# A cross-attention and FP4 feed-forward layer on one core: the down projection in three f32r products, and the low part of x subtracted by GpSimd

## What is computed

```python
def fp4_quant_dequant(x):             # blocks of 16 along the last dim
    scale = max(abs(block)) / 6.0 ; xn = block / scale
    return _GRID[searchsorted(_MID, abs(xn))] * sign(xn) * scale
def fp4_linear(x, w):
    return einsum('bsk,nk->bsn', fp4_quant_dequant(x), fp4_quant_dequant(w))

x = x + attention(layernorm(x), ctx, ctx, bias, mask, in_proj, out_proj)
x = x + fp4_linear(silu(fp4_linear(ln, w_gate)) * fp4_linear(ln, w_up), w_down)   # ln = layernorm(x)
```

## Time and profile before

| | |
|---|---|
| median of 3 runs | 930.79 us |
| the profiled execution | 930.9 us, span 928.9 us |
| PE busy | 883.6 us, 95% |
| DVE busy | 710.6 us, 76% |
| ACT busy | 617.8 us, 67% |
| POOL busy | 534.8 us, 58% |
| granted TensorE clock | 0.993 on average |

### The profile page before, as it was taken

The page is one execution under the profiler, slowest core; times in us unless marked ns, Lnnn a source line. Parts: engine busy times, 40 slices in busy tenths (PEclk is TensorE's granted clock), DMA queues, the critical chain, the costliest instruction groups (busy, mean ns, idle before and its releaser), DMA issues.

```text
span 928.9 us, 20211 instructions
## 1 busy us (share of the span) xinstructions
PE 883.6 (95%) x6772; PEld 706.7 (76%) x6772; DVE 710.6 (76%) x1866; ACT 617.8 (67%) x1119; POOL 534.8 (58%) x501
## 2 busy tenths in 40 slices
PE   5699999999999999999999999999889999999997
PEld 5577777787777777777787777777568888888886
DVE  3868678677677776776776679899579999989984
ACT  2377677777677776777776777787755555555542
POOL 5677867776696687677678557875203222222222
PEclk9799999999999999999999999999999999999999
DMA  6577334442442534344243343610000000000000
GB/s 193 150 221 205 113 72 126 103 117 71 114 116 60 146 86 102 98 100 132 74 115 103 72 134 73 174 35 1 1 1 12 18 18 19 21 17 17 18 18 29
DMA packets 50796, 76.50 MB, mean 82 GB/s; under 512 B 5264, under 2 KB 22032, under 8 KB 50704
## 3 DMA queue, kind: packets, MB, share of 16 engines
q1 hardware_dynamic: 50448, 75.06, 29.9%
q10 hardware_dynamic: 256, 0.26, 0.1%
HBM read 45.16 MB, written 29.36 MB: 80 GB/s over the span
## 4 chain that ended last, share of the span: by engine, by line
PE 79%; ACT 6%; issue 6%; DVE 4%; POOL 2%; DMA 2%; SPq 1%; ACTq 0%; DVEq 0%
PE psum L1233 26%; PE psum L1377 11%; PE psum L1331 11%; PE psum L1584 9%; PE psum L1569 4%; PE psum L1568 4%; PE psum L1567 4%; PE psum L1295 3%; PE psum L1255 2%; ACT att L776 2%; DVE att L1089 2%; PE psum L1261 2%; ACT att L783 1%; PE psum L1272 1%; ACT att L727 1%
## 5 line engine op out<-in xcount | busy, mean ns | idle before, releaser
L1089 DVE CUSTOM_DVE_ANT_0 att<-psum,att 128x512 f32<-128x512 f32 x512 | 341.7, 686 | 143.3 <-PE psum L1331 141.4
L618 POOL TENSOR_TENSOR att<-att,neg_max 128x512 f32<-128x512 f32 x308 | 322.4, 1057 | 172.8 <-DVE neg_max L1089 170.4
L1233 PE MATMUL psum<-ident,att 128*128 128x128 f32 x2576 | 380.8, 276 | 25.2 <-ACT att L776 8.2
L1233 PEld LDWEIGHTS psum<-ident,att 128*128 128x128 f32 x2576 | 311.6, 142 | 93.0 <-ACT att L776 30.2
L776 ACT ACTIVATE att<-psum 128x512 f32<-128x512 f32 x512 | 298.3, 599 | 117.7 <-PE psum L1233 113.4
L1331 PE MATMUL psum<-stack 128*128 128x512 f32 x512 | 251.2, 492 | 10.5 <-DMA stack<-q_hl 7.2
L783 ACT ACTIVATE att<-att,neg_max 128x512 f32<-128x512 f32 x204 | 147.2, 722 | 13.4 <-DVE neg_max L1089 13.4
L701 POOL TENSOR_TENSOR att<-att 128x704 f32<-128x704 f32 x32 | 61.8, 1931 | 162.8 <-DVE att L1211 162.8
L1331 PEld LDWEIGHTS psum<-stack 128*128 128x128 f32 x512 | 97.8, 191 | 43.9 <-issue 32.3
L1377 PE MATMUL psum<-att 128*32 128x256 f32 x2048 | 123.8, 382 | 0.0
L1584 PE MATMUL psum<-att 128*128 128x256 f32 x384 | 91.7, 380 | 2.7 <-ACT att L903 2.7
(11 more groups left out here) (104 smaller groups left out, 1066.3 us busy)
## 6 DMA issues: line engine op xcount, KB each, us to landing
stack<-qk_planes SPq DMA_DIRECT2D x124, 192.0 KB, 3.9
qk_planes<-k_hl SPq DMA_DIRECT2D x48, 256.0 KB
qk_planes<-q_hl SPq DMA_DIRECT2D x48, 256.0 KB
att<-in_fside_1xSxS_dram SPq DMA_DIRECT2D x32, 256.0 KB, 2.8
att<-in_ctx_dram SPq DMA_DIRECT2D x8, 512.0 KB, 7.4
out_dram<-att SPq DMA_DIRECT2D x32, 128.0 KB, 1.7
x<-in_x_dram SPq DMA_DIRECT2D x1, 2560.0 KB, 13.5
x<-in_x_dram SPq DMA_DIRECT2D x3, 512.0 KB, 6.5
```

The costliest lines, as they stand in the source:

```text
L618: pool.tensor_tensor(prob[:, slot, :], prob[:, slot, :], neg_max[:, slot:slot + 1].to_broadcast([P, S]), ALU.subtract).then_inc(less_pool, 1)
L1089: dve.tensor_tensor_reduce(out=prob[:, slot, :], in0=ps_score[:, SCORE_BANK[2 * S_ + r], :], in1=bias_m[:, tt, :], scale=-1.0, scalar=BIG, ...
L1233: return pe.transpose(out_, in_, ident[:, :])
```

## The change

Down is now made in three f32r products like gate and up: 18 matmuls of 128x256 in place of six float32 chunks. For that, h gets a high and a low part: ACT copies PSUM twice, once rounded (into `hqT_hl`, in a slot of `stack` that attention has left), once in float32 (`f_hT`), and POOL subtracts. The down weights get a low part too, made by DVE (`weights_low`) from the three down pieces, in the place of `k_hl` and a longer `kv_hl`. The matmul with the negated identity is gone; instead ACT copies transposed x twice and POOL subtracts as well. PE transposes x of the next tile in the middle of gate and up, behind twelve of the 18 matmuls. The ring `prob` goes from 13 to 12 slots. Names of semaphores, buffer sizes and asserts are left out of the diff.

```diff
-    RING = 13
+    RING = 12
...
+        w_dn_high = kv_hl[:, AT_DN:AT_DN + IC * E].rearrange("p (c e) -> p c e", c=IC)
+        w_dn_low2 = kv_hl[:, AT_DN + IC * E:].rearrange("p (c e) -> p c e", c=2)
+        w_dn_low4 = k_hl.rearrange("p a s -> p (a s)").rearrange("p (c e) -> p c e", c=IC - 2)
+        def w_dn_low(c):
+            return w_dn_low4[:, c, :] if c < IC - 2 else w_dn_low2[:, c - IC + 2, :]
...
+        f_hT = cut(IC * P)
...
+        f_x32 = cut(E)
...
+        hqT_hl = stack[:, (2 * N_OCT - 1) % SLOTS, :, :, :].rearrange("p x k s -> p (x k s)").rearrange(
+            "p (i j n) -> p i j n", i=2, j=2)
...
-            pool.memset(w_dnT[:, IC - 1, :], 0.0).then_inc(vv_zero, 1)
+            pool.memset(kv_hl[:, 4 * EC * S:].bitcast(F32), 0.0).then_inc(vv_zero, 1)
...
             batches(pool, body)
+            def step(n, par):
+                m = n - 3
+                if live(m):
+                    pool.wait_ge(fhT_taken, m + 1)
+                    wait(pool, fdn_ready, m - 1)
+                    pool.tensor_tensor(hqT_hl[:, 1 - par, 1, :], f_hT, hqT_hl[:, 1 - par, 0, :].bitcast(F32),
+                                       ALU.subtract).then_inc(fhlow_ready, 1)
+                m = n - 2
+                if live(m):
+                    pool.wait_ge(fhd_ready, m + 1)
+                    if isinstance(m, int) and m == 0:
+                        pool.wait_ge(fgu_ready, 1)
+                        pool.memset(f_hq[:, :, I:IC * P], 0.0)
+                    wait(pool, fhT_ready, m - 1)
+                    pool.tensor_tensor(blocks(f_hq[:, par, 0:I]), blocks(f_hu), spread(f_s[:, 1 - par, 0:NHB], NHB),
+                                       ALU.mult).then_inc(fhq_ready, 1)
+                m = n + 1
+                if live(m):
+                    pool.wait_ge(fxT_taken, m + 1)
+                    pool.tensor_tensor(f_xqT_low[:, 1 - par, :, :].rearrange("p c t -> p (c t)"), f_x32,
+                                       f_xqT_high[:, 1 - par, :, :].rearrange("p c t -> p (c t)").bitcast(F32),
+                                       ALU.subtract).then_inc(fxlow_ready, 1)
+            ffn_head(step, -2, -1, 0)
             rstd2_of(B - 1)
-            def step(n, par):
-                m = n - 2
-                if not live(m):
-                    return
-                pool.wait_ge(fhd_ready, m + 1)
-                if isinstance(m, int) and m == 0:
-                    pool.wait_ge(fgu_ready, 1)
-                    pool.memset(f_hq[:, :, I:IC * P], 0.0)
-                wait(pool, fhT_ready, m - 1)
-                pool.tensor_tensor(blocks(f_hq[:, par, 0:I]), blocks(f_hu), spread(f_s[:, 1 - par, 0:NHB], NHB),
-                                   ALU.mult).then_inc(fhq_ready, 1)
-            ffn_loop(pool, step)
+            ffn_loop(pool, step, 1)
...
-                act.activation(f_xqT_high[:, par, :, :], ps_x[:, 0:E].rearrange("p (c t) -> p c t", c=EC),
-                               ACT.Copy).then_inc(fxT_taken, 1)
-            def x_low(m, par):
-                act.wait_ge(fxlow_made, m + 1)
-                act.activation(f_xqT_low[:, par, :, :], ps_x[:, 0:E].rearrange("p (c t) -> p c t", c=EC),
-                               ACT.Copy).then_inc(fxlow_ready, 1)
+                act.activation(f_xqT_high[:, par, :, :], ps_x[:, 0:E].rearrange("p (c t) -> p c t", c=EC), ACT.Copy)
+                wait(act, fxlow_ready, m)
+                act.activation(f_x32, ps_x[:, 0:E], ACT.Copy).then_inc(fxT_taken, 1)
...
-                    act.activation(f_hqT[:, 1 - par, :, :].rearrange("p c t -> p (c t)"), ps_h[:, 0:IC * P], ACT.Copy).then_inc(fhT_taken, 1)
+                    if isinstance(m, int) and m == 0:
+                        act.wait_ge(score_ready, TILES * N_OCT)
+                    act.activation(hqT_hl[:, 1 - par, 0, :], ps_h[:, 0:IC * P], ACT.Copy)
+                    wait(act, fhlow_ready, m)
+                    act.activation(f_hT, ps_h[:, 0:IC * P], ACT.Copy).then_inc(fhT_taken, 1)
...
+                if g == 2:
+                    src = bank.rearrange("p (c n) -> p c n", c=2)
+                    if m < IC - 2:
+                        dve.wait_ge(k_plane, 48 * N_OCT)
+                        dve.tensor_tensor(w_dn_low4[:, m:m + 2, :], src, w_dn_high[:, m:m + 2, :].bitcast(F32), ALU.subtract).then_inc(gw_low, 1)
+                    else:
+                        dve.tensor_tensor(w_dn_low2[:, 0, :], src[:, 0, :], w_dn_high[:, m, :].bitcast(F32), ALU.subtract)
+                        dve.tensor_tensor(w_dn_low2[0:ILAST, 1, :], src[0:ILAST, 1, :], w_dn_high[0:ILAST, m + 1, :].bitcast(F32),
+                                          ALU.subtract).then_inc(gw_low, 1)
+                    return
...
+            def x_transposes(m, par):
+                if not live(m):
+                    return
+                pe.wait_ge(fxq_ready, m + 1)
+                wait(pe, fxT_taken, m)
+                for c in range(EC):
+                    last = transposes(ps_x[:, c * P:(c + 1) * P], f_xq[:, 1 - par, c * P:(c + 1) * P])
+                last.then_inc(fxT_ready, 1)
             def ffn_step(n, par):
                 m = n - 3
                 if live(m):
@@ -1569,32 +1606,24 @@
                             last = pe.matmul(ps_gu[:, c0:c1], f_xqT_low[:, par, c, :], w_gu_high[:, c, c0:c1], start=False, stop=c == EC - 1)
                         if c0 < I <= c1:
                             last.then_inc(fgate_ready, 1)
+                            x_transposes(n + 1, par)
                     last.then_inc(fgu_ready, 1)
-                m = n + 1
-                if live(m):
-                    pe.wait_ge(fxq_ready, m + 1)
-                    wait(pe, fxlow_ready, m)
-                    for c in range(EC):
-                        last = pe.matmul(ps_x[:, c * P:(c + 1) * P], f_xq[:, 1 - par, c * P:(c + 1) * P], ident[:, :],
-                                         start=c == 0, stop=False, is_transpose=True, skip_group_check=True)
-                    last.then_inc(fxT_ready, 1)
-                def down(m, chunks):
-                    for c in chunks:
-                        last = pe.matmul(ps_y[:, 1 - par, :], f_hqT[:, 1 - par, c, :], w_dnT[:, c, :],
-                                         start=c == 0, stop=c == IC - 1)
-                    return last
+                elif live(n + 1):
+                    x_transposes(n + 1, par)
                 if live(n - 3):
                     pe.wait_ge(fhT_taken, n - 2)
                     wait(pe, fout_ready, n - 3)
-                    down(n - 3, range(0, IC // 2))
-                if live(m):
-                    pe.wait_ge(fxT_taken, m + 1)
-                    pe.matmul(ps_x[:, 0:E], neg_ident[:, :], f_xqT_high[:, 1 - par, :, :], start=False, stop=True,
-                              skip_group_check=True).then_inc(fxlow_made, 1)
-                if live(n - 3):
-                    down(n - 3, range(IC // 2, IC)).then_inc(fdn_ready, 1)
+                    for c in range(IC):
+                        high = hqT_hl[:, 1 - par, 0, c * P:(c + 1) * P]
+                        pe.matmul(ps_y[:, 1 - par, :], high, w_dn_high[:, c, :], start=c == 0, stop=False)
+                        pe.matmul(ps_y[:, 1 - par, :], high, w_dn_low(c), start=False, stop=False)
+                    pe.wait_ge(fhlow_ready, n - 2)
+                    for c in range(IC):
+                        last = pe.matmul(ps_y[:, 1 - par, :], hqT_hl[:, 1 - par, 1, c * P:(c + 1) * P], w_dn_high[:, c, :],
+                                         start=False, stop=c == IC - 1)
+                    last.then_inc(fdn_ready, 1)
```

More of the change, by code:

```diff
@@ L86, in xattn_ffn @@
         neg_half = sb("neg_half", [P, NT])
-        att = sb("att", [P, 28352])
+        att = sb("att", [P, 26816])
         used = [0]
@@ L121, in xattn_ffn @@
         oT = cut(EC, S)
-        at_w_dn = used[0]
-        w_dnT = cut(IC, E)
+        w_qT = cut(EC, E)
         w_outT = cut(EC, E)
@@ L126, in xattn_ffn @@
         bo_bc = cut(E)
-        w_qT = att[:, at_w_dn:at_w_dn + EC * E].rearrange("p (c e) -> p c e", c=EC)
         w_nat = probT.rearrange("p a b c d -> p (a b c d)")[:, 0:8 * E].rearrange("p (c e) -> p c e", c=8)
@@ L142, in xattn_ffn @@
         mean_var_b = sb("mean_var_b", [P, NT, 2])
-        neg_ident = sb("neg_ident", [P, P], F32R)
         var_eps2 = sb("var_eps2", [P, NT])
@@ L158, in xattn_ffn @@
         w_gu_high = stack[:, (2 * N_OCT - 3) % SLOTS, :, :, :].rearrange("p x k s -> p (x k s)")[:, 0:EC * GU].rearrange("p (c n) -> p c n", c=EC)
-        kv_hl = sb("kv_hl", [P, 4 * EC * S], F32R)
+        AT_DN = EC * GU
+        kv_hl = sb("kv_hl", [P, AT_DN + (IC + 2) * E], F32R)
         ctxT_high, ctxT_low, w_kv_high, w_kv_low = (
             kv_hl[:, i * EC * S:(i + 1) * EC * S].rearrange("p (c s) -> p c s", c=EC) for i in range(4))
-        assert 2 * E == S and EC * GU <= 4 * EC * S
+        assert 2 * E == S and 4 * EC * S <= AT_DN + (IC + 2) * E
```

(27 more changed lines are left out.)

2 lines of the change are left out of this document (removed).

## The result

The changed kernel takes 962.17 us (median of 4 runs, 961.45 to 962.32), the kernel before 930.84 us on the same chip (4 runs, 929.17 to 931.35). The ratio is 1.0338 [1.032, 1.0356]: 31 us slower. The forecast was 959.0 us, in a range of 938 to 972, with a chance of 0.88 for slower. The profiled execution took 962.24 us, its span 960.4 us.

What follows compares the result with a forecast made beforehand. The prediction took the chain through PE, ACT, POOL and DVE, 8.24 us a tile, as the bound. 930.9 us plus 23.2 for 28 tiles, 3.7, 1.9 and -1 gave 958.7, stated as 959, range 938 to 972.

Steps and rivals of the forecast that it cites:

- The mechanism: Feed-forward loop: POOL and DVE instructions with two SBUF operands hold each other, making the tile 8.24 us, 0.83 more.
- The chain, step by step: Feed-forward tile, from h's transposes over ACT's copies, POOL's subtraction, DVE and POOL's multiplication to the next transposes: 8.24 us.
- PE's sum: PE's own work in a feed-forward tile: 7.41 - 0.31 - 2.40 + 2.16 + 0.09 = 6.95 us.
- the split into 0.31 for L1594 and 2.40 for the float32 products: PE's down stretch: time freed by removing the negated-identity matmul (0.31 us) and the float32 down (2.40 us).
- the 0.09 us for a change of kind: PE, gate and up: transposes of x placed among the matmuls cost one more switch of kind, 0.09 us a tile.
- 28 x 0.83 = 23.2: Feed-forward loop: 28 tiles at the full pitch, each 0.83 us longer than before, add 23.2 us.
- The tail: Last three tiles: DVE has little to do, the chain alone counts, 5.73 us instead of 4.51 a tile: +3.7 us.
- The last batch of attention: DVE, 99% busy there, also makes the down weights' low parts: +1.9 us (0 to 2.2).
- The start of the pipeline: Start of the feed-forward pipeline: loses PE's waits around L1594, gains POOL's for x: -1 us (-2 to +2).
- A quicker subtraction: Rival: POOL's subtraction for h takes 1.51 us or meets more DVE PSUM instructions; tile 7.91 us, total 948.5; chance 0.14.
- More blocking of x's subtraction: Rival: x's subtraction and three short DVE instructions also delay each other; DVE 8.6 us a tile, total 969; chance 0.09.
- No blocking: Third rival: DVE and POOL do not hold each other in feed-forward; PE decides with 6.95 us, total 922.6; chance 0.09.

Runs made afterwards that it cites:

- The PSUM operand: The changed kernel with DVE's two rounding instructions of h (L1229, L1238) reading their second operand from PSUM instead of SBUF: 939.08 us, ratio 1.0096.
- the bystander: The kernel before plus one POOL subtraction of 768 scratch columns a tile, ahead of the multiplication, whose result nobody waits for: 946.56 us, ratio 1.0179.
- the half subtraction: The changed kernel with POOL's subtraction for h over 384 of the 768 columns: 938.11 us, ratio 1.0085.
- the x part alone: The kernel before with x's low part subtracted by POOL and x transposed amid gate and up; down stays float32, ring of 13: 927.14 us, ratio 0.9968.
- the first and the fifth experiment: First: the PSUM operand on the changed kernel, 939.08 us. Fifth: the bystander on the kernel before, 946.56 us.
- with the multiplication first: The changed kernel with POOL's multiplication put ahead of its subtraction for h: 954.25 us, ratio 1.0267.

## Why the prediction came out right

**The mechanism** was the forecast one in the full loop. PE's work did fall, the chain through ACT, POOL and DVE became longer than it, and L1229 stood behind POOL's subtraction. The PSUM operand and the bystander show the exclusion in two ways that leave a longer chain alone no room; the half subtraction shows that the held stretch follows POOL's length. No run takes every collision out (with the PSUM operand a tile still takes 7.54 us), so that PE's own sum would be reached without them is not shown.

**The chain, step by step**: 0.91 (0.86 forecast) to ACT's first copy, 0.71, 0.81, 0.07, POOL's 1.85 (1.84), 0.75 from there to the end of L1229 and 1.14 on to the end of L1238 (together 1.89; 1.86 forecast), 2.05 to the end of the multiplication, 0.05 to PE. That is 8.34 us, 0.10 over the forecast 8.24, half of it between the transposes and ACT.

**PE's sum.** Down in 18 f32r matmuls: the first twelve start at 761.11 and the last six at 762.53, 0.118 us each, so 2.14 us (2.16 forecast):

```profile
761.11 0.28 PE L1620 MATMUL psum<-kv_hl,stack 128*128 128x256 f32 x1
...
762.53 0.88 PE L1624 MATMUL psum<-kv_hl,stack 128*128 128x256 f32 x6
```

The whole of PE's tile without its wait is 4.83 us from the transposes of h (764.63) to down (769.46) and 2.14 of down, 6.97 us (6.95 forecast). The total was right, but two of its readings were not.

The first is the split into 0.31 for L1594 and 2.40 for the float32 products: the products take 2.59, and L1594 added 0.12. The kernel before shows it itself. In its last tiles, where no x is left to transpose, L1594 is missing and down takes 912.70 - 910.11 = 2.59 us; and in the earlier trace rows the sixth float32 matmul has hardly begun (the second of the two from 748.25 on) when the record of L1594 starts:

```profile
910.11 2.75 PE L1584 MATMUL psum<-att 128*128 128x256 f32 x12
912.70 0.82 PE L1233 MATMUL psum<-ident,att 128*128 128x128 f32 x6
...
748.25 0.59 PE L1584 MATMUL psum<-att 128*128 128x256 f32 x2
```

The float32 matmuls start 0.216 us apart (2.59 / 12), so the sixth starts at 748.47 and L1594 already at 748.49. From 748.47 to the next float32 one (748.80) it is 0.33 us for both together, 0.12 more than for one alone. For the full change the sum is the same; for the x part alone it is the difference between 0.3 and 0.1 us a tile.

The second is the 0.09 us for a change of kind where the transposes of x stand amid gate and up. It isn't there: from the transposes of x (768.20) to the second matmul behind them (768.59) it is 0.39 us for two transposes and one narrow matmul, and the same three took 0.39 before (L1569 at 746.99 to L1584 at 747.38). Instead PE is slower just after its wait: from the transposes of h to the second wide matmul 1.02 us (764.63 to 765.65), where it was 0.89 (742.68 to 743.57). That the total came within 0.02 us is thus in part luck.

**The sum in us.** The first 27 intervals between starts of the multiplication took 225.0 us after and 197.8 before: +27.2, where the forecast had 28 x 0.83 = 23.2. Of the 4.0 us, 2.7 are the 0.10 us of the chain over 27 tiles. The rest is that the count took the pitch of before as 7.41 us from the first tile on, while the first three took 6.32, 6.85 and 6.85 us (8.01, 8.34 and 8.33 after), which weighs more than the one tile counted too many. The tail came to +4.4 (+3.7): +3.1 over its last four intervals and +1.4 behind the last multiplication. The last batch of attention lost 2.4 (1.9). The start of the pipeline gained 1.5 (1): 17.1 us in place of 17.9 from the last score to the first gate and up, 21.6 in place of 22.2 from there to the fourth. And 1.0 us fewer went by before the last batch, which the forecast did not have; the first batch took 75.9 us in this one execution and 77.1 to 77.2 in the profiles of the kernel before and of all experiments. Why is open; it is not the ring, which has 12 slots in seven of those. Together 27.2 + 4.4 + 2.4 - 1.5 - 1.0 = 31.5, the difference between the two spans; the forecast was 27.8. The errors in the loop, the tail and the last batch all pointed the same way.

**The tail.** Its number was near, its picture was not. The forecast let DVE have little to do in the last tiles and POOL's two instructions follow each other at once, 5.73 us a tile. From one start of down to the next the last two took 7.20 and 6.94 us (940.69, 947.89 and 954.83). DVE is held there as well, only at another instruction, and POOL's multiplication then stands behind L1242 as in the full loop:

```profile
940.72 1.83 POOL L706 TENSOR_TENSOR stack<-att,stack 128x768 fp32r<-128x768 f32 x1 [2.55 <-ACT att L926]
943.37 1.96 POOL L716 TENSOR_TENSOR att<-att 128x704 f32<-128x704 f32 x1 [0.83 <-DVE att L1238]
...
940.78 2.52 DVE L1238 SCALAR_TENSOR_TENSOR att<-att 128x704 f32<-128x704 f32 x1
...
940.00:945.00 5.00, 2.67 (x18) 2.27 (x18) 4.39 (x4) 1.43 (x2) 3.45 (x2) 1.00 0.08 26
945.00:948.00 3.00, 1.01 (x7) 0.75 (x7) 1.78 (x2) 1.51 (x2) 0.43 (x2) 0.69 0.13 44
948.00:950.00 2.00, 2.00 (x10) 2.00 (x11) 0.00 (x0) 0.00 (x0) 2.00 (x2) 0.50 0.00 0
```

The last three lines are the windows view, with the granted TensorE clock as the third number from the end. PE was busy for 2.67 of 5 us and then for 1.01 of 3, and the clock went to 0.50, that is 1.2 GHz; the products of down there start 0.21 us apart in place of 0.12. An estimate from the rows: POOL's multiplication ended at 951.08 and the transposes of h, behind those slow products, began at 951.90; from them to the next down it was 2.93 us, 2.50 a tile earlier. That makes 1.2 us of the 4.4. The forecast had no term for the clock.

**The rivals.** A quicker subtraction: it took 1.85 us where it came first, and up to 2.48 us in a tile where it came second to DVE. More blocking of x's subtraction: 0.73 us, undisturbed, right behind the multiplication, at DVE's reductions with one operand. No blocking: excluded by the first and the fifth experiment. The rule quoted ahead of the result from the Trainium skill (Advanced Engine Details and Errata, VectorE Performance Modes), that two-port instructions of VectorE are the ones that block, would have given that third rival; read as complete it does not hold here: L1229 is no faster when free than a PSUM reader (0.88 and 0.89 us for 704 columns), and it lost 1.50 us. The trace agrees with another page of the Trainium skill, the GPSIMD Engine Reference (Specifications), which names instructions with two SBUF inputs beside the two-port modes. It gives no size; here the size is the rest of the other's instruction.

## What to carry to other kernels

A low-part subtraction is not free on an idle GpSimd: VectorE's instructions with two SBUF operands stand until it is nearly over, even if nobody needs its result. Subtractions and multiplications of two SBUF tensors were tried here, and no other kind of GpSimd instruction. Before work is moved there, list what VectorE does in that time, and put it beside instructions with one operand or with one in PSUM. In a profile the sign is a VectorE instruction whose busy time is far over its usual one, not idle time; compare its shortest and its mean.

Price an instruction by what its neighbours do without it, not by its own slot: that of L1594 was 0.31 us, and its removal was worth 0.12. In a row of matmuls of different types, compare two stretches from start to start, with and without it.

## What the hardware showed that was not expected

- GpSimd's subtraction of 768 columns took 1.47 us with both operands and the result in one place, and 1.83 to 1.85 us with two different operands and an f32r result. Which of the two differences it is was not tried apart.
- Freeing one VectorE instruction moved the collision to the next one with two SBUF operands (L1234, 1.13 us in place of 0.41).
- GpSimd is held too: with the multiplication first, L721 took 0.92 us in place of 0.73 where it started beside L1198 (762.84; L1198 ran from 762.57 to 763.16), and it held L1210 in its turn, 0.70 us in place of 0.41.
- The record of an f32r matmul behind a float32 one starts early: L1594 0.03 us behind a float32 matmul whose fellows start 0.216 us apart. Its slot holds most of that matmul's time.
- PE's granted clock fell to 0.50 near the end of the changed kernel (948 to 950 us); in the last tiles of the kernel before it was 1.00 from 915 to 928 us.
